# Row maxima of causal attention scores: two full key blocks as one shared score plus the positive part of a difference

## The chip, the cores and the metric

One core of a Trainium2 chip runs the whole program. Its engines are TensorE (PE in the profile, PEld for its weight loads), VectorE (DVE), ScalarE (ACT), GpSimd (POOL) and SyncE (SP, which here issues DMAs). The metric is the device time of one execution in microseconds; the median of three runs is compared.

## The reference

Four layers run on 4096 rows of 128 numbers: a message-passing layer with a recurrent layer behind it, a neighbour average, and a transformer layer with causal attention and a mixture of eight experts. The change is in the attention of the last layer. It has 4 query heads and 2 key heads of width 32, and 4096 positions:

```python
q = q * cos + _rotate_half(q) * sin
k = k * cos + _rotate_half(k) * sin
k = jnp.repeat(k, NREP, axis=1)
scores = jnp.einsum('bhtd,bhsd->bhts', q, k) / jnp.sqrt(jnp.float32(HD))
scores = jnp.where(causal[None, None], scores, jnp.float32(-1e+30))
att = jax.nn.softmax(scores, axis=-1)
```

The softmax needs, for each query and head, the largest score over all keys up to the query.

## The kernel before, in words

The program is a row of phases, each closed before the next begins. Three of them matter here.

`split_heads` (L808) projects the rows to queries and keys, turns them by the position tables, and leaves each head in 16-bit pieces: `T.qs[h]` holds query rows as high, low and high part (96 rows), `T.ks[h]` the key rows as high, high and low part, so that one matmul over 96 rows gives a score of nearly 32-bit accuracy. It runs over 8 groups `g` of 512 positions. For each group PE projects, DVE multiplies by the cosine and sine tables (`turn(g)`, L941 to L949), POOL adds the two products (L988, L990), ACT rounds to 16 bits (L1011, L1013), and DVE subtracts to get the low parts (`lows(g - 1)`, L954 to L962, one group behind). The pieces are put in their rows by DMAs: SP loads the two tables of a group (L861, L862) and issues eight placements of query high parts (L869), ACT those of the key high parts and query low parts (L1016, L1002), POOL those of the key low parts (L983). SP's program is a fixed sequence: the tables of group `g + 2`, which wait for `turn` of group `g`, then the eight placements of group `g`, and so on.

`make_masks` (L1643) follows, with a few instructions.

`row_maxima` (L1025) finds the maxima. Queries go in 32 tiles of 128 (four tiles `k` to each group `g`), and for each tile and each head `h` the keys from the start to the tile's own group go in chunks `c` of two blocks of 512 keys. One (group, tile, head, chunk) is a unit; there are 320, in a fixed order, and each engine's program follows that order. In a unit PE writes one score block of 128 x 512 for each key block (L1066), and for the block of the tile's own group it adds the mask by a further matmul (L1069). DVE then reduces the unit's 512 or 1024 columns to one maximum (L1081). Three PSUM buffers `sc` of two blocks each go round: PE may begin unit `u` when unit `u - 3` is reduced. After the last chunk of the last head of a tile, DVE makes the tile's negated maxima and splits them in two 16-bit halves (L1087, L1092, L1095). Once per group PE transposes these (`flatten`, L1053; that of the previous group comes before tile 1 of a group) and ACT copies the result into two further rows of `T.qs` (L1116). In this phase ACT does nothing else, and POOL works only in its first microseconds (L1106 to L1109).

The last chunk of each unit list is the only one with a mask: in an even group it holds one block (512 columns, two matmuls), in an odd group two blocks (1024 columns, three matmuls). All chunks before it are two full blocks of earlier groups: 1024 columns and two matmuls. There are none of these in groups 0 and 1, one per tile and head in groups 2 and 3, two in groups 4 and 5 and three in groups 6 and 7, 192 of the 320 units in all.

`attend` (L1120) comes next and uses the same queries and keys with exponentials.

Of the kernel before, what the change touches and what calls it, by code (L numbers as in the profile page):

```python
# [807 lines left out]
def split_heads(nc, T):  # L808
# [6 lines left out]
    with Phase(nc, "heads") as ph:  # L815
# [12 lines left out]
        k, ks = ([ph.sb(f"{n}{i}", [P, G]) for i in range(2)] for n in ("k", "ks"))  # L828
# [23 lines left out]
        def _(sp):  # L852
# [52 lines left out]
        def _(dve):  # L905
# [27 lines left out]
            def turn(g):  # L933
                b = g % 2
                dve.wait_ge(tables[b], 32 * (g // 2 + 1))
                dve.wait_ge(q_projected, g + 1)
                if g >= 2:
                    dve.wait_ge(q_low_ready, g - 1)
                    dve.wait_ge(q_high_ready, g - 1)
                    dve.wait_ge(q_ready, g - 1)  # L940
                nc.vector.tensor_tensor(q[b][:, :], q_plain[b][:, :], cos[b][:, :], ALU.mult)  # L941
                nc.vector.tensor_tensor(qs[b][:, :], q_turned[b][:, :], sin[b][:, :], ALU.mult).then_inc(q_turned_by, 1)
                dve.wait_ge(k_projected, g + 1)
                if g >= 2:
                    dve.wait_ge(k_low_ready, g - 1)
                    dve.wait_ge(k_high_ready, g - 1)
                    dve.wait_ge(k_ready, g - 1)
                nc.vector.tensor_tensor(k[b][:, :], k_plain[:, :], cos[b][:, :], ALU.mult)
                nc.vector.tensor_tensor(ks[b][:, :], k_turned[:, :], sin[b][:, :], ALU.mult).then_inc(k_turned_by, 1)  # L949

            def lows(g):
# [10 lines left out]
                nc.vector.tensor_tensor(k_low[b][:, :], k[b][:, :], k_high[b][:, :], ALU.subtract).then_inc(k_low_ready, 1)  # L962
# [8 lines left out]
        def _(pool):  # L971
# [13 lines left out]
            for g in range(NG):  # L985
# [4 lines left out]
                nc.gpsimd.tensor_tensor(k[b][:, :], k[b][:, :], ks[b][:, :], ALU.add).then_inc(k_ready, 1)  # L990
# [5 lines left out]
        def _(act):  # L996
# [7 lines left out]
            for g in range(NG):  # L1004
# [8 lines left out]
                nc.scalar.copy(k_high[b][:, :], k[b][:, :]).then_inc(k_high_ready, 1)  # L1013
# [8 lines left out]
MAX_UNIT = 2.0 ** 15  # L1022


def row_maxima(nc, T):  # L1025
# [3 lines left out]
    with Phase(nc, "maxima") as ph:  # L1029
        sc = [ph.ps(f"sc{i}", [P, 2, G]) for i in range(3)]  # L1030
        flat = ph.ps("flat", [2, NHEAD, G], F16)
        part = ph.sb("part", [P, 2, NHEAD, NG // 2])
# [6 lines left out]
        units = [(g, k, h, c) for g in range(NG) for k in range(TPG) for h in range(NHEAD) for c in range(g // 2 + 1)]  # L1039
        tiles_done = [sum(NHEAD * (g // 2 + 1) * TPG for g in range(t // TPG)) + NHEAD * (t // TPG // 2 + 1) * (t % TPG + 1)  # L1040
# [3 lines left out]
        def _(pe):  # L1044
# [12 lines left out]
            for u, (g, k, h, c) in enumerate(units):  # L1057
# [4 lines left out]
                t = g * TPG + k  # L1062
                for j in range(min(2, g + 1 - 2 * c)):
# [48 lines left out]
        def _(act):  # L1112
            for g in range(NG):
# [3 lines left out]
                last.then_inc(placed, 1)  # L1117

# [554 lines left out]
def program(nc, D, out):  # L1673
    T = Tensors()
    Phase.used.clear()
    with ExitStack() as ctx:
# [41 lines left out]
        with ExitStack() as third:  # L1718
            def sb3(name, shape, dt=F32):
                return third.enter_context(nc.sbuf_tensor(name, shape, dt))  # L1720
# [7 lines left out]
            T.ks = [sb3(f"ks{h}", [P, N], F16) for h in range(NKV)]  # L1728
            T.score_unit = sb3("score_unit", [P, 1])
# [76 lines left out]
```

## Time and profile before

| | us |
|---|---|
| median of 3 runs | 7872.52 |
| lowest and highest run | 7867.58, 7874.14 |
| the profiled execution, its own time | 7870.33 |
| span of that execution in the profile | 7868.3 |
| VectorE busy in it | 5390.5 |
| TensorE busy | 4613.6 |
| ScalarE busy | 2829.4 |

Times in the profile count from the start of the span. The recurrent layer takes most of the span; `split_heads` begins at 6312, `row_maxima` runs from 6393 to 6752 and `attend` follows it. Busy time is the union of an engine's instructions. An instruction's duration is longer than the distance to the next one where two of them overlap, so both are read below: a group's mean gives the duration, a timeline the distance.

### The profile page before, as it was taken

To read this page: it belongs to the slowest core of one execution; us is meant where nothing else is said; L and a number is where in the kernel's file an instruction comes from. 1 tells how busy PE (TensorE), PEld (TensorE's weight loads), DVE (VectorE), ACT (ScalarE), POOL (GpSimd) and SP (SyncE) were. 2 spreads that over 40 slices of the span, in tenths; PEclk is the share of its full clock that TensorE was granted. 3 is DMA by queue.
4 is the path that set the end of the run, shared out by engine and by line. 5 is a ranking of instruction groups with operands and counts; after the bars stand their busy time and mean duration, and the time that the engine had idled before them with its cause. 6 is when DMAs were issued, how large, how long until landed. Compare 5 with 4: busy or idle time off the path is not lost. (4 is left out here: it accounts for less than half of the span.)

```text
span 7868.3 us, 179097 instructions
## 1 busy us (share of the span) xinstructions
PE 4613.6 (59%) x57632; PEld 3119.7 (40%) x57632; DVE 5390.5 (69%) x30690; ACT 2829.4 (36%) x14714; POOL 217.7 (3%) x504
## 2 busy tenths in 40 slices
PE   4555555555555555555555555555446868788799
PEld 3444444444444444444444444444333421344344
DVE  7666666666666666666666666666646679788544
ACT  3333333333333333333333333333320010488333
POOL 0000000000000000000000000000000020000011
PEclk6555555555555555555555555555558975799799
DMA  1000000000000000000000000000004610000000
GB/s 44 14 12 14 14 12 14 14 13 14 14 14 12 14 14 13 14 14 12 14 14 12 14 14 12 14 14 12 2 2 144 200 48 0 2 1 1 24 4 5
DMA packets 93261, 164.29 MB, mean 21 GB/s; under 512 B 8711, under 2 KB 23087, under 8 KB 92337
## 3 DMA queue, kind: packets, MB, share of 16 engines
q1 hardware_dynamic: 89009, 150.47, 6.1%
q8 instruction: 442, 7.24, 0.4%
q14 instruction: 482, 3.95, 0.2%
q10 hardware_dynamic: 2816, 2.10, 0.1%
q0 software_dynamic: 512, 0.53, 0.0%
HBM read 146.25 MB, written 2.10 MB: 19 GB/s over the span
## 5 line engine op out<-in xcount | busy, mean ns | idle before, releaser
L431 PE MATMUL lstm_gates<-lstm_h_parts,lstm_wrec 128*128 128x1 f16 x36864 | 2074.0, 170 | 2822.8 <-DVE lstm_h_parts L576 2814.6
L431 PEld LDWEIGHTS lstm_gates<-lstm_h_parts,lstm_wrec 128*128 128x128 f16 x36864 | 1615.6, 107 | 3425.4 <-DVE lstm_h_parts L576 3414.3
L487 ACT ACTIVATE lstm_tanhs<-lstm_gates 128x3 f32<-128x3 f32 x4096 | 707.5, 173 | 2726.2 <-PE lstm_gates L431 2726.0
L431 PE MATMUL lstm_gate_o<-lstm_h_parts,lstm_wrec 128*128 128x1 f16 x12288 | 1440.7, 165 | 0.0
L576 DVE SCALAR_TENSOR_TENSOR lstm_h_parts<-lstm_tanh_o,lstm_c_pair 128x1 f16<-128x1 f32 x4096 | 645.5, 158 | 912.8 <-ACT lstm_c_pair L493 912.8
L571 DVE SCALAR_TENSOR_TENSOR lstm_terms<-lstm_tanhs 128x2 f32<-128x2 f32 x4096 | 655.1, 160 | 765.9 <-ACT lstm_tanhs L487 546.1
L595 DVE RECIPROCAL lstm_rec<-lstm_dist 128x52 f32<-128x52 f32 (+1 forms) x2560 | 1171.6, 462 | 4.2 <-issue 4.2
L493 ACT ACTIVATE lstm_c_pair<-lstm_c_pair 128x1 f32<-128x1 f32 x4096 | 639.0, 156 | 951.4 <-DVE lstm_terms L571 951.4
L431 PEld LDWEIGHTS lstm_gate_o<-lstm_h_parts,lstm_wrec 128*128 128x128 f16 x12288 | 961.2, 104 | 0.0
L454 PE MATMUL lstm_acc<-msg,lstm_wt 128*128 128x128 f32 x2048 | 780.9, 488 | 38.2 <-DVE lstm_wt L603 38.2
L582 DVE TENSOR_TENSOR lstm_h_parts<-hid_t,lstm_h_parts 128x1 f16<-128x1 f32 x4096 | 667.5, 163 | 179.9 <-DVE hid_t L578 13.1
L490 ACT ACTIVATE lstm_tanh_o<-lstm_gate_o 128x1 f32<-128x1 f32 x4096 | 679.9, 166 | 0.0
L585 DVE TENSOR_SCALAR lstm_tanhs<-lstm_c_pair 128x1 f32<-128x1 f32 x4096 | 622.1, 152 | 7.4 <-issue 7.4
L578 DVE SCALAR_TENSOR_TENSOR hid_t<-lstm_tanh_o,lstm_c_pair 128x1 f32<-128x1 f32 x4096 | 608.3, 149 | 0.0
L571 DVE DVE_READ_ACCUMULATOR lstm_terms<-lstm_tanhs 128x1 f32 x4096 | 580.1, 142 | 0.0
L454 PEld LDWEIGHTS lstm_acc<-msg,lstm_wt 128*128 128x128 f32 x2048 | 512.2, 312 | 41.0 <-DVE lstm_wt L603 21.4
L1081 DVE TENSOR_REDUCE maxima_part<-maxima_sc 128x1 f32<-128x1024 f32 (+1 forms) x320 | 331.2, 1109 | 6.5 <-PE maxima_sc L1069 6.1
L1303 DVE TENSOR_TENSOR attend_low<-xn_t,attend_high 128x1024 f16<-128x1024 f32 (+1 forms) x288 | 324.2, 1162 | 6.3 <-ACT attend_high L1259 1.4
L1254 ACT ACTIVATE xn_t<-attend_sc 128x1024 f32<-128x1024 f32 (+1 forms) x288 | 281.3, 983 | 117.9 <-PE attend_sc L1184 71.1
L1066 PE MATMUL maxima_sc<-ks,qs 96*128 96x512 f16 x576 | 263.7, 565 | 68.8 <-DVE maxima_part L1081 38.8
L603 DVE SCALAR_TENSOR_TENSOR lstm_wt<-lstm_dist,lstm_sens 128x128 f32<-128x128 f32 x1024 | 294.9, 291 | 4.6 <-issue 4.6
L1486 PE MATMUL experts_up<-experts_f,experts_w 128*128 128x512 f16 (+1 forms) x1152 | 280.3, 389 | 23.2 <-DVE experts_hidden L1606 22.6
(260 smaller groups left out, 4626.0 us busy)
## 6 DMA issues: line engine op xcount, KB each, us to landing
lstm_ring<-in_adj SPq DMA_DIRECT2D x256, 256.0 KB, 2.7
gnn_ring<-in_adj SPq DMA_DIRECT2D x64, 1024.0 KB, 5.2
w<-in_w SPq DMA_DIRECT2D x2, 1364.0 KB, 9.5
heads_cos<-in_cos SPq DMA_DIRECT2D x8, 256.0 KB, 3.1
heads_sin<-in_sin SPq DMA_DIRECT2D x8, 256.0 KB, 3.5
qs<-heads_q_high SPq DMA_DIRECT2D x64, 32.0 KB, 2.3
out<-x SPq DMA_DIRECT2D x8, 256.0 KB, 2.3
ks<-heads_k_high ACTq DMA_DIRECT2D x16, 64.0 KB, 2.6
```

The costliest lines, as they stand in the source:

```text
L431: return nc.tensor.matmul(o, wrec[:, w, g, :], h_parts[:, (n - 1) % NH, k:k + 1], start=False, stop=True, skip_group_check=True)
L454: nc.tensor.matmul(acc[t % 2][:, :], wt[:, q % 2, r, :], T.msg[:, (q % QPT) * QUAD + r, :], start=first, stop=True, skip_group_check=True) ...
L487: nc.scalar.activation(tanhs[:, 0:3], gates[t % 2][:, i, :], ACT.Tanh, scale=unscale).then_inc(tanhs_ready, 1)
L490: nc.scalar.activation(tanh_o[:, :], gate_o[t % 2][:, i:i + 1], ACT.Tanh, scale=unscale).then_inc(tanh_o_ready, 1)
L493: nc.scalar.activation(tanh_c, c_twice, ACT.Tanh, scale=0.5).then_inc(tanh_c_ready, 1)
L571: nc.vector.scalar_tensor_tensor(out=terms[:, :], in0=tanhs[:, 0:2], scalar=1.0, in1=tanhs[:, 2:4], op0=ALU.add, op1=ALU.mult, accum_out=c ...
L576: nc.vector.scalar_tensor_tensor(out=h_parts[:, n % NH, 0:1], in0=tanh_o[:, :], scalar=1.0, in1=tanh_c, op0=ALU.add, op1=ALU.mult).then_in ...
L578: nc.vector.scalar_tensor_tensor(out=T.hid_t[:, n:n + 1], in0=tanh_o[:, :], scalar=1.0, in1=tanh_c, op0=ALU.add, op1=ALU.mult).then_inc(fu ...
L582: nc.vector.tensor_tensor(h_parts[:, n % NH, 1:2], T.hid_t[:, n:n + 1], h_parts[:, n % NH, 0:1], ALU.subtract).then_inc(low_ready, 1)
L585: nc.vector.tensor_scalar(tanhs[:, 3:4], c_twice, 0.5, None, ALU.mult).then_inc(c_kept, 1)
L595: nc.vector.reciprocal(rec[:, q % 2, c], dist[:, q % 3, c]).then_inc(rec_ready, 1)
L1081: nc.vector.reduce_max(part[:, k % 2, h, c:c + 1], sc[u % 3][:, 0:w, :].rearrange("p a s -> p (a s)"), AX.X).then_inc(reduced, 1)
```

## The change

Of two full key blocks `a` and `b` the larger of two scores is written as `sb + max(0, q(ka - kb))`. `split_heads` makes the key differences `d = ka - kb` of the block pairs (0,1), (2,3) and (4,5), splits them in a 16-bit high and low part and places them in a new tensor `T.kd`, laid out as `T.ks`. To have the key of the group before at hand, the key buffer goes from 2 to 3. In `row_maxima` PE scores, in the 192 full units, the difference block and the block `b`; ACT takes the positive part of the first into one of three new buffers `more`; DVE adds the second to it and takes the maximum in one instruction. The masked units stay as they were. ACT's copies of the flattened maxima are put between its new instructions.

In `split_heads`:

```diff
+            def place_difference(p):
+                c = slice(p * G, (p + 1) * G)
+                sp.wait_ge(d_low_ready, p + 1)
+                for h in range(NKV):
+                    sp.dma_start(T.kd[h][0:2 * HD, c], d_high[2 * h * HD:2 * (h + 1) * HD, :]).then_inc(d_placed, 16)
+                    sp.dma_start(T.kd[h][rows(2), c], d_low[rows(2 * h), :]).then_inc(d_placed, 16)
             for g in range(NG):
                 if g + 2 < NG:
                     load_tables(g + 2)
                 place(g)
+                if g % 2 == 0 and 1 <= g // 2 <= NPAIR:
+                    place_difference(g // 2 - 1)
+            sp.wait_ge(d_placed, 16 * 2 * NKV * NPAIR)
...
-                nc.vector.tensor_tensor(k[b][:, :], k_plain[:, :], cos[b][:, :], ALU.mult)
+                nc.vector.tensor_tensor(k[g % 3][:, :], k_plain[:, :], cos[b][:, :], ALU.mult)
...
+                p = g // 2
+                if b and p < NPAIR:
+                    if p >= 1:
+                        dve.wait_ge(d_placed, 16 * 2 * NKV * p)
+                    nc.vector.tensor_tensor(d[:, :], k[(g - 1) % 3][:, :], k[g % 3][:, :], ALU.subtract).then_inc(d_ready, 1)
+                    dve.wait_ge(d_ready, p + 1)
+                    nc.vector.tensor_copy(d_high[:, :], d[:, :]).then_inc(d_high_ready, 1)
+                    dve.wait_ge(d_high_ready, p + 1)
+                    nc.vector.tensor_tensor(d_low[:, :], d[:, :], d_high[:, :], ALU.subtract).then_inc(d_low_ready, 1)
```

In `row_maxima` (`NPAIR` is 3, `LOWEST` is -3e38):

```diff
+        doubled = [2 * c + 1 < g for g, k, h, c in units]
...
+                if doubled[u]:
+                    nc.tensor.matmul(sc[u % 3][:, 0, :], T.qs[h][0:K, t * P:(t + 1) * P], T.kd[h // 2][0:K, c * G:(c + 1) * G],
+                                     start=True, stop=True)
+                    nc.tensor.matmul(sc[u % 3][:, 1, :], T.qs[h][0:K, t * P:(t + 1) * P],
+                                     T.ks[h // 2][0:K, (2 * c + 1) * G:(2 * c + 2) * G],
+                                     start=True, stop=True).then_inc(scored, 1)
+                    continue
...
-                nc.vector.reduce_max(part[:, k % 2, h, c:c + 1], sc[u % 3][:, 0:w, :].rearrange("p a s -> p (a s)"),
-                                     AX.X).then_inc(reduced, 1)
+                if doubled[u]:
+                    dve.wait_ge(more_ready, sum(doubled[:u + 1]))
+                    m = more[(sum(doubled[:u + 1]) - 1) % 3][:, :]
+                    nc.vector.tensor_tensor_reduce(out=m, in0=m, in1=sc[u % 3][:, 1, :], scale=1.0, scalar=LOWEST, op0=ALU.add, op1=ALU.max,
+                                                   accum_out=part[:, k % 2, h, c:c + 1]).then_inc(reduced, 1)
+                else:
+                    nc.vector.reduce_max(part[:, k % 2, h, c:c + 1], sc[u % 3][:, 0:w, :].rearrange("p a s -> p (a s)"),
+                                         AX.X).then_inc(reduced, 1)
...
+            pairs = [u for u in range(len(units)) if doubled[u]]
+            place(0)
+            for n, u in enumerate(pairs):
+                g, k, h, c = units[u]
+                if (k, h, c) == (2, 0, 0):
+                    place(g - 1)
+                act.wait_ge(scored, u + 1)
+                if n >= 3:
+                    act.wait_ge(reduced, pairs[n - 3] + 1)
+                nc.scalar.activation(more[n % 3][:, :], sc[u % 3][:, 0, :], ACT.Relu).then_inc(more_ready, 1)
+            place(NG - 1)
```

`place(g)` is ACT's old loop body: the wait for `flatten(g)` and four copies.

## Rows read from the trace of the kernel before

**Rows 1.** The page: busy time of each engine, its share of the span, instructions.
```profile
PE 4613.6 (59%) x57632; PEld 3119.7 (40%) x57632; DVE 5390.5 (69%) x30690; ACT 2829.4 (36%) x14714; POOL 217.7 (3%) x504
```
**Rows 2.** Stretches of row_maxima, groups 1, 2, 3, 6, 7: length, busy PE, PEld, DVE, ACT, POOL (instructions), clock, DMA.
```profile
6411.20:6431.60 20.40, 14.70 (x64) 4.50 (x62) 20.00 (x28) 2.00 (x4) 0.00 (x0) 0.92 0.00 1
6431.60:6461.60 30.00, 23.99 (x82) 5.94 (x81) 29.52 (x43) 2.00 (x4) 0.00 (x0) 0.77 0.00 0
6461.60:6500.70 39.10, 31.97 (x97) 7.93 (x95) 38.51 (x47) 2.00 (x4) 0.00 (x0) 0.70 0.00 1
...
6605.60:6672.00 66.40, 59.56 (x144) 11.23 (x145) 65.99 (x77) 2.00 (x4) 0.00 (x0) 0.55 0.00 0
6672.00:6747.70 75.70, 66.33 (x157) 13.77 (x155) 74.84 (x79) 2.00 (x4) 0.00 (x0) 0.55 0.00 0
```
**Rows 3.** Who waited for whom, 6410 to 6748: us in total, times, longest.
```profile
ACT qs L1116 <- PE maxima_flat L1053: 302.5, 7, 66.9
PEld maxima_sc L1066 <- DVE maxima_part L1081: 242.3, 287, 1.8
...
DVE maxima_part L1081 <- PE maxima_sc L1066: 0.4, 1, 0.4
```
**Rows 4.** DVE's timeline in row_maxima: start, us, line, shapes, count (merged).
```profile
6398.92 2.48 DVE L1081 TENSOR_REDUCE maxima_part<-maxima_sc 128x1 f32<-128x512 f32 x4
...
6411.16 3.49 DVE L1081 TENSOR_REDUCE maxima_part<-maxima_sc 128x1 f32<-128x1024 f32 x3
```
**Rows 5.** Groups by line and shape, 6300 to 7400: count, busy us, mean ns, idle before.
```profile
L1081 DVE TENSOR_REDUCE maxima_part<-maxima_sc 128x1 f32<-128x1024 f32 x256 | 295.2, 1216 | 0.4 <-PE maxima_sc L1066 0.4
...
L1254 ACT ACTIVATE xn_t<-attend_sc 128x512 f32<-128x512 f32 x32 | 19.1, 598 | 7.4 <-PE attend_sc L1188 7.4
...
L1301 DVE CAST attend_high<-xn_t 128x512 f16<-128x512 f32 x16 | 6.7, 422 | 0.0
...
L941 DVE TENSOR_TENSOR heads_q<-heads_q_plain,heads_cos 128x512 f32<-128x512 f32 x8 | 5.5, 688 | 8.7 <-DMA heads_sin<-in_sin 4.4 <-PE heads_q_turned L892 4.4
...
L962 DVE TENSOR_TENSOR heads_k_low<-heads_k,heads_k_high 128x512 f16<-128x512 f32 x8 | 5.4, 679 | 0.0
```
**Rows 6.** A timeline in the recurrent layer: an instruction with an accumulator, and the next engine.
```profile
3000.40 0.16 DVE L571 SCALAR_TENSOR_TENSOR lstm_terms<-lstm_tanhs 128x2 f32<-128x2 f32 x1
3000.48 0.14 DVE L571 DVE_READ_ACCUMULATOR lstm_terms<-lstm_tanhs 128x1 f32 x1
3000.66 0.16 ACT L493 ACTIVATE lstm_c_pair<-lstm_c_pair 128x1 f32<-128x1 f32 x1 [0.23 <-DVE lstm_terms L571]
```
**Rows 7.** Timeline of group 0, DVE behind PE (0.50 clock), and one unit of group 1.
```profile
6394.74 0.69 DVE L1081 TENSOR_REDUCE maxima_part<-maxima_sc 128x1 f32<-128x512 f32 x1 [0.16 <-PE maxima_sc L1069]
...
6395.60 0.69 DVE L1081 TENSOR_REDUCE maxima_part<-maxima_sc 128x1 f32<-128x512 f32 x1 [0.16 <-PE maxima_sc L1069]
...
6412.44 0.60 PE L1066 MATMUL maxima_sc<-ks,qs 96*128 96x512 f16 x2 [0.73 <-DVE maxima_part L1081]
```
**Rows 8.** Timelines around the flattening, groups 1 and 7: PE, ACT, DVE.
```profile
6413.20 1.05 PE L1053 MATMUL maxima_flat<-ident,maxima_halves 128*2 128x128 f16 x16
...
6414.29 2.00 ACT L1116 COPY qs<-maxima_flat 2x512 f16<-2x512 f16 x4 [38.29 <-PE maxima_flat L1053]
...
6690.96 0.17 DVE L1095 SCALAR_TENSOR_TENSOR maxima_halves<-maxima_neg,maxima_halves 128x4 f16<-128x4 f32 x1
6691.51 2.36 DVE L1081 TENSOR_REDUCE maxima_part<-maxima_sc 128x1 f32<-128x1024 f32 x2 [0.38 <-PE maxima_sc L1066]
...
6747.80 1.87 PE L1053 MATMUL maxima_flat<-ident,maxima_halves 128*2 128x128 f16 x16 [2.54 <-DVE maxima_halves L1095]
```
**Rows 9.** split_heads: SP's only wait for another engine, SP's last issues, DVE's first wait for tables, the next phase.
```profile
SPq L860 <- DVE heads_ks L949: 19.4, 1, 19.4
...
6368.64 15.40 SPq L869 DMA_DIRECT2D qs<-heads_q_high  x24
...
6359.25 0.69 DVE L941 TENSOR_TENSOR heads_q<-heads_q_plain,heads_cos 128x512 f32<-128x512 f32 x1 [2.23 <-DMA heads_sin<-in_sin]
...
6386.04 0.11 DVE L1652 MEMSET ident<- 128x64 uint32 x1 [8.08 <-PEq L62]
```

More of the change, by code:

```diff
@@ L827, in split_heads @@
         q, qs = ([ph.sb(f"{n}{i}", [P, G]) for i in range(2)] for n in ("q", "qs"))
-        k, ks = ([ph.sb(f"{n}{i}", [P, G]) for i in range(2)] for n in ("k", "ks"))
+        k, ks = ([ph.sb(f"{n}{i}", [P, G]) for i in range(m)] for n, m in (("k", 3), ("ks", 2)))
+        d = ph.sb("d", [P, G])
+        d_high, d_low = ph.sb("d_high", [P, G], F16), ph.sb("d_low", [P, G], F16)
+        d_ready, d_high_ready, d_low_ready, d_placed = (ph.sem(n) for n in ("d_ready", "d_high_ready", "d_low_ready", "d_placed"))
         q_high, q_low = ([ph.sb(f"{n}{i}", [P, G], F16) for i in range(2)] for n in ("q_high", "q_low"))
@@ L944, in turn @@
                 if g >= 2:
-                    dve.wait_ge(k_low_ready, g - 1)
-                    dve.wait_ge(k_high_ready, g - 1)
                     dve.wait_ge(k_ready, g - 1)
-                nc.vector.tensor_tensor(k[b][:, :], k_plain[:, :], cos[b][:, :], ALU.mult)
+                if g >= 3:
+                    dve.wait_ge(k_low_ready, g - 2)
+                    dve.wait_ge(k_high_ready, g - 2)
+                    dve.wait_ge(d_ready, min((g - 1) // 2, NPAIR))
+                nc.vector.tensor_tensor(k[g % 3][:, :], k_plain[:, :], cos[b][:, :], ALU.mult)
                 nc.vector.tensor_tensor(ks[b][:, :], k_turned[:, :], sin[b][:, :], ALU.mult).then_inc(k_turned_by, 1)
@@ L961, in lows @@
                 dve.wait_ge(k_high_ready, g + 1)
-                nc.vector.tensor_tensor(k_low[b][:, :], k[b][:, :], k_high[b][:, :], ALU.subtract).then_inc(k_low_ready, 1)
+                nc.vector.tensor_tensor(k_low[b][:, :], k[g % 3][:, :], k_high[b][:, :], ALU.subtract).then_inc(k_low_ready, 1)
+                p = g // 2
[7 more added lines that the diff above has]
+                    nc.vector.tensor_tensor(d_low[:, :], d[:, :], d_high[:, :], ALU.subtract).then_inc(d_low_ready, 1)
             for g in range(NG):
@@ L989, in _ @@
                 pool.wait_ge(k_turned_by, g + 1)
-                nc.gpsimd.tensor_tensor(k[b][:, :], k[b][:, :], ks[b][:, :], ALU.add).then_inc(k_ready, 1)
+                nc.gpsimd.tensor_tensor(k[g % 3][:, :], k[g % 3][:, :], ks[b][:, :], ALU.add).then_inc(k_ready, 1)
                 if g >= 1:
@@ L1012, in _ @@
                 act.wait_ge(k_ready, g + 1)
-                nc.scalar.copy(k_high[b][:, :], k[b][:, :]).then_inc(k_high_ready, 1)
+                nc.scalar.copy(k_high[b][:, :], k[g % 3][:, :]).then_inc(k_high_ready, 1)
                 act.wait_ge(k_high_ready, g + 1)
@@ L1022 @@
 MAX_UNIT = 2.0 ** 15
+NPAIR = (NG - 1) // 2
+LOWEST = -3e38
 def row_maxima(nc, T):
@@ L1031, in row_maxima @@
         flat = ph.ps("flat", [2, NHEAD, G], F16)
+        more = [ph.sb(f"more{i}", [P, G]) for i in range(3)]
+        more_ready = ph.sem("more_ready")
         part = ph.sb("part", [P, 2, NHEAD, NG // 2])
@@ L1112, in _, with place @@
         def _(act):
-            for g in range(NG):
+            def place(g):
                 act.wait_ge(flat_ready, g + 1)
@@ L1728, in program @@
             T.ks = [sb3(f"ks{h}", [P, N], F16) for h in range(NKV)]
+            T.kd = [sb3(f"kd{h}", [P, NPAIR * G], F16) for h in range(NKV)]
             T.score_unit = sb3("score_unit", [P, 1])
```

## The prediction

> **What bounds the kernel now.** Over the whole span VectorE is busiest at 69% [rows 1], but that is an average over phases with different limits, and the change touches two of them. So I read the stretches of `row_maxima`, group by group. DVE is busy for 98 to 99% of each (74.84 of 75.70 us in group 7) while ACT has four copies, 2.00 us [rows 2]. The waits say the same from the other side: between 6410 and 6748 PE's weight loads waited 242.3 us for reductions, DVE's reductions 0.4 us for PE's scores, and ACT sat idle for 302.5 us [rows 3]. VectorE sets the pace here and ScalarE is free.
>
> The second thing to see is the distance between reductions, not their duration. Three of 1024 columns end 3.49 us after the first began and one lasts 1.216 us [rows 4, 5], so the distance is (3.49 - 1.22) / 2 = **1.135 us**. Four of 512 columns take 2.48 us at 0.69 each [rows 4, 7]: distance (2.48 - 0.69) / 3 = **0.60 us**. This rebuilds group 7: per tile and head four units of 1024 columns, 16 times, 16 x 4 x 1.135 = 72.6 us, and four tile ends of about 0.6 us give 75.0 of the measured 75.7.
>
> The third is TensorE's clock: mean 0.92 in group 1, 0.77, 0.70, and 0.55 in groups 6 and 7 [rows 2], that is, first nearly always at 2.4 GHz, then mostly at 1.2. At the lower level a unit of two matmuls costs PE 0.855 us: the two reductions of group 0 that wait for PE start 6395.60 - 6394.74 = 0.86 apart, 0.43 per matmul. At the upper level two matmuls are over in 0.60 us [rows 7].
>
> In `split_heads` SP is the limit from 6335 on: its queue waited once for another engine, and its last 24 placements run to 6384 without a gap; the next phase starts at 6386, when they have landed [rows 9].
>
> **The change part by part.** *DVE in the 192 full units.* Out goes a reduction of 1024 columns at 1.135 us. In comes one instruction over 512 columns with one operand from PSUM and one from SBUF, and a maximum to hand out. No such instruction is in the trace. Nearest for its body is the product of a PSUM and an SBUF tile of that size, 0.688 us long [rows 5], which is the duration of a 512-column reduction, so I give it that one's distance, 0.60. For the maximum handed out, the nearest row is the recurrent layer's accumulator read: a second DVE instruction, begun 0.08 us after the first, 0.14 long [rows 6]. I take 0.08, the distance; the bounds are nothing (the value leaves with the body) and 0.23 (body and read both run to their ends before the next: 0.69 + 0.14 = 0.83). So 0.68 us, and 192 x (1.135 - 0.68) = **-87.4 us**, with ends -102.7 and -58.6.
>
> *ACT.* The positive part of 512 PSUM columns is priced by the exponential of that size and output type, 0.598 us [rows 5]. Bounds: 0.48 (distance of its small copies, (2.00 - 0.57) / 3 [rows 8]) and 0.62 or so. It lies under DVE's 0.68, beside it. It is no bound of its own, but DVE now waits for ACT, and ACT for PE.
>
> *The ring of three buffers.* What is late next is that chain. PE's two matmuls 0.60, ACT 0.60, DVE until its maximum is out 0.60 + 0.14 = 0.74, and three handovers of 0.04 (the read ends at 3000.62, ACT starts at 3000.66 [rows 6]) make 2.06 us, in which three units pass. Three full units at DVE's pace are 2.04, two and one masked unit of 512 columns 1.96, two and one of 1024 columns 2.50. So per tile and head the ring adds about 0.05 us in group 2, 0.1 in groups 4 and 6, 0.03 in 7 and nothing in 3 and 5: 16 x 0.28 = **+5 us**. Before, the ring was slack.
>
> *Flattening and copies.* PE's 16 transposes (1.05 us at the upper level, 1.87 at the lower) already let DVE wait 0.38 us in group 7 [rows 8]; with the ring tight I expect about 1 us each in groups 2 to 7, 0.6 more than now: **+4 us**. ACT's four copies (2.00 us) now stand between its positive parts. They begin when the last full unit of a tile is through; DVE then still has that unit (0.68), the masked one (0.60 or 1.135) and the tile's end (0.6) before it: 1.9 to 2.4 us against 2.0 for copies and 0.6 for the next positive part. 0.2 to 0.7 is uncovered, six times: **+3 us**.
>
> *The clock.* The number of matmuls is unchanged. If PE stood at the lower level throughout, groups 2 to 7 (4, 5, 6, 7, 8 and 9 matmuls per tile and head) would cost it 16 x 39 x 0.427 = 266.5 us, against 213.8 us for DVE's new units (16 times 1.28, 1.815, 1.96, 2.495, 2.64 and 3.175). So where the clock is low, PE becomes the bound: 53 us if always. Group 1, where PE does three matmuls in each 1.135 us, ran at 0.92, group 7 with nine in 4.54 us at 0.55 [rows 2]. After the change group 7 has nine in 3.2 us, nearer to group 1's work than to its own of now, so I take group 1's 0.92, which is 16% of the time at the lower level: 0.16 x 53 = **+8 us**.
>
> *`split_heads`.* SP gets 12 more placements behind the query ones. Its last 24 took 15.40 us, 0.64 each [rows 9], nothing hides them, since SP's queue is the phase's limit: **+7.7 us**, with ends of 0 (if a queue pays for the transfers, not for their number) and 15 (if the tables queued behind them come late for DVE and it costs as much again). SP's new wait for the low part finds it made; what is queued behind it, the tables of the next group but two, has waited for DVE in any case. DVE gets 3 x (0.68 + 0.42 + 0.68) = 5.3 us of differences [rows 5]; they hide behind SP, for DVE waits 4.4 us for tables in all [rows 5], 2.23 of it in group 4 [rows 9]. Without that cover they would cost up to 5 us. The third key buffer removes no wait that shows.
>
> *Sum.* -87.4 + 5 + 4 + 3 + 8 + 7.7 = -59.7 us. From the profiled execution's own 7870.3 that is 7810.6. The median of the runs lies 2.2 us above that execution, so 7812.8: **7813 us**. The unknown read cost alone moves it from about 7800 (the ring then takes back part of the gain) to 7842.
>
> **The rivals.** *The clock stays down.* PE still pauses between units, waiting for a buffer, and a clock that stays at 1.2 GHz makes PE the bound: 266.5 us and six flattenings of 1.87, 278 us for groups 2 to 7, which now last 6747.7 - 6431.6 = 316.1 us [rows 2]. That is -38, with +7.7 -30: **7842 us**, and up to 15 more with imperfect overlap. For it: groups 6 and 7 stand at 0.55 with PE busy for 88 to 90% of the time [rows 2]. Against it: a bound PE would pause no more, and group 1 has 0.92. The Trainium skill's page "TensorE: Matmul & The Clock Gate", section "A second HAM failure mode: psum-queue depth-cycling", says that short idles between matmul groups that go round PSUM buffers let the clock fall and rise again; groups 2 and 3 with 0.77 and 0.70 agree with that. Chance 0.17.
>
> *The new instruction goes through its columns at half the rate* (slower). Two sources, an addition and a running maximum might take two cycles a column. Then its body has the distance of 1024 columns, 1.135, and the read's 0.08 on top: 192 x 0.08 = +15, and with the placements' 7.7 +23: **7895 us**. The change turns to a loss from a distance of about 1.135 - 7.7 / 192 = 1.095 us. Against it: the two-source product and the one-source reduction of 512 columns take the same 0.68 to 0.69 us [rows 5, 7]; for it: neither of those does both. Chance 0.09. The Trainium skill's "Vector Engine (DVE) Microarchitecture Reference", section "Points that are easy to get wrong", halves the rate of a form with two 32-bit sources in SBUF; here one is in PSUM, so by its letter the rule does not bite, and no row here shows the case.
>
> **How the numbers follow.** The forecast, with its bounds, has 0.74. A measurement of this kernel can tell about 0.2%, 16 us, from no change, so faster means under 7857. That holds for the forecast (0.73; 0.01 within) and most of the clock's case (0.14; 0.03 within); of the half rate 0.08 is slower and 0.01 within. Faster 0.87, same 0.05, slower 0.08. The range goes from 7785 (read for nothing, clock at the upper level, the small terms gone: -102.7 + 10 + 7.7 = -85) to 7853, which takes in most of the clock's case and leaves out the half rate.
>
> **What would show it.** Right: `split_heads` ends about 8 us later; groups 2 to 7 last some 248 us in place of 316; the new DVE instruction stands 0.68 to 0.72 us apart; clock of 0.9 there; DVE's idle time is put down to ACT. Wrong: distances over 0.85 us, or a clock near 0.55 with DVE waiting for PE behind ACT, or ACT's positive part at over 0.7 us, which would make the ring, not DVE, the bound.

## The result and the profile after

| | before | after |
|---|---|---|
| median of six runs each, us | 7870.85 | 7798.76 |
| lowest and highest run | 7865.7, 7874.14 | 7796.64, 7806.16 |
| span of the profiled execution | 7868.3 | 7794.7 |

The ratio is 0.991, with a 95% interval from 0.9898 to 0.9923. The forecast was 7813 us, with a range from 7785 to 7853: right in sign and range, and 14 us too cautious.

The first question is where the 73.6 us of span went. I take the limits from VectorE's timeline: `split_heads` from its first reduction (6314.91 before, 6312.10 after) to the first instruction of `make_masks`, and `row_maxima` from its first reduction to its last 16-bit half. `split_heads` went from 71.1 to 78.6 us (+7.5), `row_maxima` from 353.7 to 276.8 (-76.9), and all the rest of the program together by -4.2; over the profiles of the runs below that rest varies by 9 us (7438 to 7447, the run with sixteen extra instructions left out), so 4.2 says nothing. Inside `row_maxima`, from one group's last half to the next's:

| group | 2 | 3 | 4 | 5 | 6 | 7 | sum |
|---|---|---|---|---|---|---|---|
| before, us | 30.3 | 38.6 | 48.5 | 56.8 | 66.3 | 75.3 | 316.0 |
| after, us | 27.2 | 30.6 | 37.8 | 40.9 | 46.7 | 55.5 | 238.7 |

On the page, over the whole span, little seems to happen (to be read against [rows 1]): VectorE lost 88 us, ScalarE gained 113.

```profile
PE 4526.7 (58%) x57609; PEld 3112.5 (40%) x57632; DVE 5302.8 (68%) x30891; ACT 2942.5 (38%) x14906; POOL 217.1 (3%) x504
```

The stretches of groups 1, 2, 3, 6 and 7 answer to [rows 2], columns as there. Two things are to be seen: the clock (third from the right), which was 0.55 in groups 6 and 7 and is now 1.00 and 0.94, and DVE's busy time, which is no longer 98% everywhere. In group 2 it is 22.23 of 27.20, in group 6 42.33 of 46.80, while in group 3 it is still 30.15 of 30.60.

```profile
6416.20:6436.80 20.60, 14.42 (x66) 4.43 (x65) 20.14 (x28) 2.60 (x5) 0.00 (x0) 1.00 0.00 1
6436.80:6464.00 27.20, 22.99 (x81) 6.50 (x81) 22.23 (x61) 11.46 (x20) 0.00 (x0) 0.81 0.00 0
6464.00:6494.60 30.60, 22.85 (x94) 6.05 (x95) 30.15 (x61) 12.16 (x21) 0.00 (x0) 1.00 0.00 1
...
6573.20:6620.00 46.80, 38.83 (x142) 8.30 (x144) 42.33 (x126) 30.10 (x52) 0.00 (x0) 1.00 0.00 1
6620.00:6675.50 55.50, 41.05 (x152) 11.05 (x154) 51.13 (x124) 29.05 (x51) 0.00 (x0) 0.94 0.00 1
```

The waits between 6410 and 6690 answer to [rows 3]. PE's weight loads still wait for VectorE, but there is a new line: VectorE itself now waits for ScalarE, 53 times and 16.8 us in all.

```profile
PEld maxima_sc L1093 <- DVE maxima_part L1120: 64.0, 118, 2.0
...
DVE maxima_more L1120 <- ACT maxima_more L1171: 16.8, 53, 1.3
```

The groups by line and shape answer to [rows 5]: 192 of the 256 reductions of 1024 columns are gone, and in their place stand VectorE's new instruction (a custom operation in the profile), its accumulator read, and ScalarE's positive part at 597 ns (the exponential that served for its price took 598).

```profile
L1120 DVE CUSTOM_DVE_ANT_0 maxima_more<-maxima_more,maxima_sc 128x512 f32<-128x512 f32 x192 | 125.3, 683 | 17.3 <-ACT maxima_more L1171 16.8 <-PE maxima_sc L1095 0.4
L1171 ACT ACTIVATE maxima_more<-maxima_sc 128x512 f32<-128x512 f32 x192 | 112.8, 597 | 126.6 <-PE maxima_sc L1095 124.9 <-DVE maxima_part L1120 0.8
...
L1123 DVE TENSOR_REDUCE maxima_part<-maxima_sc 128x1 f32<-128x1024 f32 x64 | 77.0, 1219 | 0.3 <-PE maxima_sc L1105 0.3
...
L1120 DVE DVE_READ_ACCUMULATOR2_ANT maxima_part<- 128x1 f32 x192 | 15.8, 82 | 0.0
```

The distance, the number on which the prediction hung, is in VectorE's timeline of group 7 (start, duration). The three custom instructions of one tile and head start at 6661.19, 6661.81 and 6662.42: **0.61 us apart**, 0.605 over longer runs. The read begins at the same time as the next body and lies wholly beside it. This answers to [rows 4], where the distance was 1.135, and to [rows 6].

```profile
6661.19 0.69 DVE L1120 CUSTOM_DVE_ANT_0 maxima_more<-maxima_more,maxima_sc 128x512 f32<-128x512 f32 x1
6661.81 0.08 DVE L1120 DVE_READ_ACCUMULATOR2_ANT maxima_part<- 128x1 f32 x1
6661.81 0.68 DVE L1120 CUSTOM_DVE_ANT_0 maxima_more<-maxima_more,maxima_sc 128x512 f32<-128x512 f32 x1
...
6662.42 0.68 DVE L1120 CUSTOM_DVE_ANT_0 maxima_more<-maxima_more,maxima_sc 128x512 f32<-128x512 f32 x1
```

In `split_heads` the answer to [rows 9] is SP's timeline: the last four difference placements (0.64 to 0.66 from start to start) stand ahead of the last eight query placements, which end at 6388.69, and the next phase starts 2.0 us later, as before.

```profile
6381.02 0.61 SPq L878 DMA_DIRECT2D kd<-heads_d_high  x1
6381.68 0.61 SPq L879 DMA_DIRECT2D kd<-heads_d_low  x1
6382.32 0.61 SPq L878 DMA_DIRECT2D kd<-heads_d_high  x1
6382.97 0.59 SPq L879 DMA_DIRECT2D kd<-heads_d_low  x1
6383.61 5.08 SPq L872 DMA_DIRECT2D qs<-heads_q_high  x8
...
6390.70 0.11 DVE L1707 MEMSET ident<- 128x64 uint32 x1 [9.83 <-PEq L62]
```

Last, the new wait, in one turn of group 6 with the clock at its upper level (all engines, in order of time). A turn is the time from a head's first full unit to the next head's. VectorE starts the first full unit of a head at 6590.65; its maximum is out when the read ends, at 6591.35. That frees the buffer of the masked unit, and PE starts it at 6591.40. VectorE starts the second full unit at 6591.27, and its read ends at 6591.95. That frees the buffer of the next head's first full unit, and PE starts it at 6592.01: its weight load (PEld) had been waiting for VectorE. Its two matmuls are over at 6592.62. ScalarE starts at 6592.65 and needs 0.60 for the first of its three; VectorE starts the next head's first full unit at 6593.39.

```profile
6590.65 0.69 DVE L1120 CUSTOM_DVE_ANT_0 maxima_more<-maxima_more,maxima_sc 128x512 f32<-128x512 f32 x1 [0.23 <-ACT maxima_more L1171]
...
6591.27 0.68 DVE L1120 CUSTOM_DVE_ANT_0 maxima_more<-maxima_more,maxima_sc 128x512 f32<-128x512 f32 x1
...
6591.40 0.39 PE L1102 MATMUL maxima_sc<-ks,qs 96*128 96x512 f16 x1 [0.32 <-DVE maxima_part L1120]
...
6591.63 0.38 PE L1105 MATMUL maxima_sc<-future_keys,ident 128*128 128x512 bf16 x1
6591.87 0.08 DVE L1120 DVE_READ_ACCUMULATOR2_ANT maxima_part<- 128x1 f32 x1
...
6592.01 0.10 PEld L1093 LDWEIGHTS maxima_sc<-kd,qs 96*128 96x128 f16 x1 [0.49 <-DVE maxima_part L1120]
6592.01 0.39 PE L1093 MATMUL maxima_sc<-kd,qs 96*128 96x512 f16 x1
...
6592.24 0.38 PE L1095 MATMUL maxima_sc<-ks,qs 96*128 96x512 f16 x1
...
6592.65 1.81 ACT L1171 ACTIVATE maxima_more<-maxima_sc 128x512 f32<-128x512 f32 x3 [0.93 <-PE maxima_sc L1095]
...
6593.39 0.69 DVE L1120 CUSTOM_DVE_ANT_0 maxima_more<-maxima_more,maxima_sc 128x512 f32<-128x512 f32 x1 [0.23 <-ACT maxima_more L1171]
```

So a turn takes 6593.39 - 6590.65 = **2.74 us**: 0.62 to VectorE's second full unit, 0.68 until that one's maximum is out, 0.06 to PE, 0.61 for two matmuls, 0.03, 0.60 ScalarE, 0.14 to VectorE. VectorE's own work in it is 3 x 0.605 + 0.60 = 2.415. In group 4, where a head has one full unit fewer, the buffer is that of the first full unit, the 0.62 falls away, and the turn is 2.14 us against 1.81 of own work. My first theory for the experiments was that the waits which VectorE now has come from this chain (with the copies and the flattening as small extras), and the 7.5 us in `split_heads` from SP's issue time; the rivals were a chain that doesn't matter beside the clock, and transfers or VectorE's differences as the cause in `split_heads`.

### The profile page after: what moved, and what is told of

Same layout as the page of the kernel before. It is cut to its first block and busy times, and to the rows that moved or that the text cites. A ratio compares the mean times of both kernels' runs of the same rounds, so it can differ in the third digit from the quotient of the medians.

```text
span 7794.7 us, 179835 instructions
## 1 busy us (share of the span) xinstructions
PE 4526.7 (58%) x57609; PEld 3112.5 (40%) x57632; DVE 5302.8 (68%) x30891; ACT 2942.5 (38%) x14906; POOL 217.1 (3%) x504
## 5 line engine op out<-in xcount | busy, mean ns | idle before, releaser
L1309 ACT ACTIVATE xn_t<-attend_sc 128x1024 f32<-128x1024 f32 (+1 forms) x288 | 281.2, 983 | 119.1 <-PE attend_sc L1239 72.8
L1661 DVE SCALAR_TENSOR_TENSOR experts_hidden<-experts_up,experts_unscale,experts_silu 128x512 f32<-128x512 f32 (+1 forms) x192 | 143.7, 750 | 191.2 <-ACT experts_silu L1602 190.5
L502 ACT ACTIVATE lstm_dist<-lstm_ring,tiny 128x256 f32<-128x256 f32 x512 | 256.1, 503 | 7.3 <-DVE lstm_scale L555 6.5
```

## The experiments

Single profiled runs of one and the same `row_maxima` give groups 2 to 7 as 238.7, 239.9 and 236.6 us (the changed kernel twice, and the run with POOL's placements below), so differences of up to 3.3 us in that sum decide nothing; the distances in a timeline do.

**`split_heads` alone.** The differences are made and placed, the whole of `row_maxima` is that of before, and nothing reads `T.kd`. The core of it:

```diff
-                if doubled[u]:
-                    dve.wait_ge(more_ready, sum(doubled[:u + 1]))
...
+                nc.vector.reduce_max(part[:, k % 2, h, c:c + 1], sc[u % 3][:, 0:w, :].rearrange("p a s -> p (a s)"),
+                                     AX.X).then_inc(reduced, 1)
```

> The key differences are made and placed, but the maxima are found as before, so nobody reads them. Theory (SP's queue is the limit of split_heads and 12 further placements at 0.62 to 0.64 us each lie on its end): make_masks begins 7.6 us later after split_heads began than in the kernel before (before: 51 us from SP's third table load at 6334.98 to 6386.04), and row_maxima lasts what it lasted before (353.7 us from the first reduction to the last halves). Rival (the placements lie beside the others and the 7.6 us of the changed kernel come from the new waits of DVE and of row_maxima's start): under 3 us.

Measured: 7880.2 us beside 7867.8 for the kernel before on the same chip. `split_heads` took 78.3 us (+7.2), groups 2 to 7 317.5 us against 316.0. The cost of the new placements is there without any of the new work in `row_maxima`, and the gain is all in the other half of the change. The other 5 of the 12.4 us lie in phases that have not changed and within their spread. `split_heads` has a spread of its own: in the seven profiles with the new placements on SP it takes 77.9 to 81.2 us.

**One wait instead of two.** In a full unit VectorE waits for ScalarE only, which itself has waited for PE.

```diff
-                dve.wait_ge(scored, u + 1)
+                if not doubled[u]:
+                    dve.wait_ge(scored, u + 1)
```

> DVE's new instruction waits for ScalarE's positive part alone, not for the scores as well (ScalarE itself waits for both scores). Rival theory (the 0.14 to 0.17 us between ScalarE's end and DVE's start, against 0.04 in the recurrent layer, is the price of the second wait): the handover falls to about 0.05 and groups 2 to 7, 238.7 us in the changed kernel, fall by about 4 to 235. Theory (the handover is no matter of the second wait): handover 0.14 to 0.17, groups 2 to 7 within 1.5 us of 238.7.

Measured: 7804.0 us; groups 2 to 7 235.8 us, 0.8 below the lowest of the three sums named above. The time decides nothing here, but the timeline of group 6 does (ScalarE's first of three ends 0.60 after its start, at 6594.52):

```profile
6591.92 0.69 DVE L1121 CUSTOM_DVE_ANT_0 maxima_more<-maxima_more,maxima_sc 128x512 f32<-128x512 f32 x1 [0.53 <-ACT maxima_more L1172]
...
6593.92 1.81 ACT L1172 ACTIVATE maxima_more<-maxima_sc 128x512 f32<-128x512 f32 x3 [1.17 <-PE maxima_sc L1095]
...
6594.55 0.69 DVE L1121 CUSTOM_DVE_ANT_0 maxima_more<-maxima_more,maxima_sc 128x512 f32<-128x512 f32 x1
```

The handover from ScalarE to VectorE fell from 0.14 to 0.03 us, and the turn from 2.74 to 2.63. The turn shortens by just what the handover lost, which it can only do if that chain sets it. The theory that the second wait doesn't matter is refuted.

**ScalarE waits for its own block.** PE reports the difference block by itself, so ScalarE starts one matmul earlier.

```diff
                     nc.tensor.matmul(sc[u % 3][:, 0, :], T.qs[h][0:K, t * P:(t + 1) * P], T.kd[h // 2][0:K, c * G:(c + 1) * G],
-                                     start=True, stop=True)
+                                     start=True, stop=True).then_inc(diffed, 1)
...
-                act.wait_ge(scored, u + 1)
+                act.wait_ge(diffed, n + 1)
```

> ScalarE waits for the difference score alone, so that PE's second matmul leaves the chain. Theory (of the 25 us by which groups 2 to 7 exceed DVE's own work of 213.8, some 17 are the chain PE, ScalarE, DVE through three score buffers): the chain is 0.22 us shorter at the upper clock, the period of a tile and head in group 6 falls from 2.74 to about 2.52, groups 2 to 7 last about 228 us. Rival (PE's clock or the flattening and copies hold DVE up, not the chain): 237 to 239 us.

Measured: 7787.6 us beside 7867.8; groups 2 to 7 230.7 us, 6 to 9 less than the three runs of the unchanged code, more than their spread. The turn in group 6 is 6610.08 - 6607.55 = 2.53 us, 0.21 shorter, and in the turn shown above a unit's second matmul ends 0.22 behind its first (6592.62 and 6592.40), which is what left the chain:

```profile
6607.55 0.69 DVE L1120 CUSTOM_DVE_ANT_0 maxima_more<-maxima_more,maxima_sc 128x512 f32<-128x512 f32 x1
...
6610.08 0.69 DVE L1120 CUSTOM_DVE_ANT_0 maxima_more<-maxima_more,maxima_sc 128x512 f32<-128x512 f32 x1
```

**PE starts on ScalarE's release as well.** The difference block of a buffer is free once ScalarE has read it; PE may refill that half before VectorE is done with the other.

```diff
-                if u >= 3:
+                early = doubled[u] and u >= 3 and doubled[u - 3]
+                if early:
+                    pe.wait_ge(more_ready, sum(doubled[:u - 2]))
+                elif u >= 3:
                     pe.wait_ge(reduced, u - 2)
...
+                    if early:
+                        pe.wait_ge(reduced, u - 2)
```

> As the run before it, and PE writes a difference score as soon as ScalarE has read the one three units back, without waiting for DVE's reduction of that unit, where both are full units. Theory (chain through the score buffers): groups 4 and 6 lose most of what is left, groups 2 to 7 last about 224 us. Rival (clock, flattening, copies): no better than the kernel as changed, 237 to 239 us.

Measured, with the edit before it included: 7787.5 us, groups 2 to 7 230.4 us. The 224 us expected did not come: there is no gain over the run before. One part of the reason stands in the timeline of group 6, where full units follow each other at 0.85 us while the granted clock is 0.50:

```profile
6598.10 0.69 DVE L1125 CUSTOM_DVE_ANT_0 maxima_more<-maxima_more,maxima_sc 128x512 f32<-128x512 f32 x1 [0.41 <-ACT maxima_more L1176]
...
6598.95 0.69 DVE L1125 CUSTOM_DVE_ANT_0 maxima_more<-maxima_more,maxima_sc 128x512 f32<-128x512 f32 x1 [0.16 <-ACT maxima_more L1176]
...
6599.80 0.69 DVE L1125 CUSTOM_DVE_ANT_0 maxima_more<-maxima_more,maxima_sc 128x512 f32<-128x512 f32 x1 [0.16 <-ACT maxima_more L1176]
```

0.85 us for two matmuls is PE at 1.2 GHz ([rows 7] have 0.86): in such stretches no chain matters, since PE itself is the bound. The releaser named is ScalarE, because it comes last, but PE was late. In this run the clock stood at 0.81 to 0.90 in groups 2, 4, 6 and 7. Why it was lower here than in other runs isn't settled.

The other part is that the edit had less to take than expected. Where the clock stood at 1.00 it did what the theory says: in group 4 the turn fell from 1.92 us with ScalarE's own block to 1.82, VectorE's own work being 1.81 (the first full units of two heads, one behind the other):

```profile
6496.30 0.68 DVE L1125 CUSTOM_DVE_ANT_0 maxima_more<-maxima_more,maxima_sc 128x512 f32<-128x512 f32 x1
...
6498.11 0.68 DVE L1125 CUSTOM_DVE_ANT_0 maxima_more<-maxima_more,maxima_sc 128x512 f32<-128x512 f32 x1
```

In group 6 it fell from 2.53 to 2.43 or 2.52, and in group 7 it stayed at 3.06, since the chain there runs by way of a masked unit, for which PE still waits for VectorE. Twelve turns in group 4 and four in group 6 at 0.10 each make an estimated 1.6 us, too little to be seen in the sum beside slow turns.

**Copies spread out.** The four copies of a flattening go one by one between the positive parts of tile 2, the changed kernel otherwise.

```diff
-                if (k, h, c) == (2, 0, 0):
-                    place(g - 1)
+                if k == 2 and c == 0:
+                    place_head(g - 1, h)
```

> ScalarE's four copies of the flattened maxima are done one before each head's first positive part in the third tile of a group, not all four before the first. Theory (four copies in a row make DVE wait 0.8 us in groups 2, 4 and 6 and up to 0.3 in group 7): groups 2 to 7 fall by 2 to 3 us from 238.7. Rival (ScalarE has no room for any copy, and the wait only moves from one place to four): within 1 us of 238.7.

Measured: 7796.3 us beside 7873.7; groups 2 to 7 233.2 us, 3.5 to 6.8 less than the three runs of the unchanged code. In the changed kernel VectorE lost 0.86 us behind the copies in groups 2, 4 and 6 and 0.33 in group 7. Now ScalarE's timeline shows each copy where it was idle before, and these losses are 0.07. That makes 2.6 us, as expected; the rest of the fall from 238.7 is not shown to be the copies' (the mean clock was 0.98 here and 0.95 there).

```profile
6592.27 1.81 ACT L1176 ACTIVATE maxima_more<-maxima_sc 128x512 f32<-128x512 f32 x3 [0.93 <-PE maxima_sc L1095]
6594.10 0.57 ACT L1159 COPY qs<-maxima_flat 2x512 f16<-2x512 f16 x1
6595.01 1.81 ACT L1176 ACTIVATE maxima_more<-maxima_sc 128x512 f32<-128x512 f32 x3 [0.34 <-PE maxima_sc L1095]
```

**POOL places the differences.** The twelve placements move from SP's program to POOL's, behind its low key parts.

```diff
-                    sp.dma_start(T.kd[h][0:2 * HD, c], d_high[2 * h * HD:2 * (h + 1) * HD, :]).then_inc(d_placed, 16)
-                    sp.dma_start(T.kd[h][rows(2), c], d_low[rows(2 * h), :]).then_inc(d_placed, 16)
+                    pool.dma_start(T.kd[h][0:2 * HD, c], d_high[2 * h * HD:2 * (h + 1) * HD, :]).then_inc(d_placed, 16)
+                    pool.dma_start(T.kd[h][rows(2), c], d_low[rows(2 * h), :]).then_inc(d_placed, 16)
```

> The 12 placements of key differences are issued by POOL behind its key placements, not by SP. Theory (SP's queue is the limit, POOL's has room): make_masks begins 7 to 8 us earlier than in the kernel as changed, as early as before the change within 1 us; row_maxima is as in the changed kernel, 277 us. Rival (POOL's additions of queries come late behind its wait for the difference, and DVE, PE and ScalarE with them): split_heads gains under 3 us or loses.

Measured: 7792.6 us; `split_heads` 74.4 us, 4.2 less than in the changed kernel but 3.2 more than before, where "within 1 us" was expected. SP's last issue ends at 6384.44, 70.1 us after the phase's first reduction (69.1 before, 76.6 in the changed kernel), so SP's time is back. But the next phase starts 4.2 us after that and not 2.0. The timeline of all engines shows who came late instead:

```profile
6376.71 0.50 POOL L1005 DMA_DIRECT2D kd<-heads_d_low  x1
...
6377.23 1.27 POOL L1010 TENSOR_TENSOR heads_q<-heads_q,heads_qs 128x512 f32<-128x512 f32 x1
...
6378.61 0.62 ACT L1035 CAST heads_q_high<-heads_q 128x512 f16<-128x512 f32 x1 [5.94 <-POOL heads_q L1010]
...
6381.60 5.12 ACTq L1026 DMA_DIRECT2D qs<-heads_q_low  x8
...
6388.66 0.11 DVE L1707 MEMSET ident<- 128x64 uint32 x1 [6.25 <-PEq L62]
```

POOL's additions of the last group stand behind its four placements, ScalarE's rounding behind those additions, and ScalarE's last eight placements behind that: they end at 6386.72, and 1.94 us later the next phase starts. The bound had moved from SP's queue to ScalarE's. Neither forecast held: the gain lies between the theory's 7 to 8 us and the rival's 3, and the late additions are the rival's.

**All of these together** (ScalarE's own block, PE's early start, copies spread out, POOL's placements); the diff is that of the four.

> ScalarE waits for its own block alone, PE writes difference scores early, the copies are spread and POOL issues the placements. Theory: the gains add up: split_heads 7.6 us shorter, groups 2 to 7 at about 222 us, in all 7775 to 7780 us. Rival (each only moves the wait to the next thing): over 7788 us.

Measured: 7777.2 us beside 7873.7, as the theory said; groups 2 to 7 222.2 us. `split_heads` took 74.4 us, 4.2 less than in the changed kernel in place of 7.6, as with POOL's placements alone. What PE's early start adds to the 222.2 no run without it shows. VectorE's own work there is 213.8: per tile and head 1.205, 1.74, 1.81, 2.345, 2.415 and 2.95 us at the paces 0.605, 0.60 and 1.135, 16 times, and 24 tile ends of 0.6. VectorE's wait for ScalarE has gone from 16.8 to 0.6 us:

```profile
DVE maxima_more L1125 <- PE maxima_sc L1100: 1.0, 3, 0.4
DVE maxima_more L1125 <- ACT maxima_more L1181: 0.6, 4, 0.2
```

**The disputed price by itself.** Behind the end of `row_maxima`, in the version with all edits and the later placements of the next run, VectorE gets four more instructions each of four forms: a sum, a sum with its maximum handed out, and both again with `more[1]` in place of the PSUM tile. The first two:

```diff
+            for e in range(4):
+                nc.vector.tensor_tensor(extra[e][:, :], more[0][:, :], sc[2][:, 1, :], ALU.add).then_inc(priced, 1)
+            dve.wait_ge(priced, 4)
+            for e in range(4):
+                nc.vector.tensor_tensor_reduce(out=extra[e][:, :], in0=more[0][:, :], in1=sc[2][:, 1, :], scale=1.0,
+                                               scalar=LOWEST, op0=ALU.add, op1=ALU.max, accum_out=most[:, e:e + 1]).then_inc(priced, 1)
```

> Sixteen extra DVE instructions of 512 columns stand at the end of the maxima, four of each form, and only the distance between their starts is read. First theory (the accumulator read costs no distance, the body keeps the pace of 0.60): the sum of an SBUF and a PSUM tile without a maximum stands 0.60 us apart, and the same with the maximum handed out 0.60 to 0.61. Second theory (the read does cost its 0.08, and the body by itself is faster): without the maximum 0.52 to 0.53 apart, with it 0.60 to 0.61. For both sources in SBUF, the rule of half rate would give 1.1 us apart with a maximum, full rate 0.60. The time as a whole should stand 9 to 12 us above the run beside it.

Measured, in VectorE's timeline: the plain sums take 2.47 for four, so (2.47 - 0.69) / 3 = 0.59 us apart; with the maximum handed out the starts run from 6658.73 to 6660.56 in three steps, 0.61 apart; with both sources in SBUF from 6661.29 to 6663.13, 0.61, and the plain sum of these 0.60 ((2.50 - 0.69) / 3).

```profile
6656.22 2.47 DVE L1150 TENSOR_TENSOR maxima_extra<-maxima_more,maxima_sc 128x512 f32<-128x512 f32 x4
6658.73 0.69 DVE L1153 CUSTOM_DVE_ANT_0 maxima_extra<-maxima_more,maxima_sc 128x512 f32<-128x512 f32 x1
...
6660.56 0.68 DVE L1153 CUSTOM_DVE_ANT_0 maxima_extra<-maxima_more,maxima_sc 128x512 f32<-128x512 f32 x1
...
6661.29 0.69 DVE L1157 CUSTOM_DVE_ANT_0 maxima_extra<-maxima_more 128x512 f32<-128x512 f32 x1
...
6663.13 0.68 DVE L1157 CUSTOM_DVE_ANT_0 maxima_extra<-maxima_more 128x512 f32<-128x512 f32 x1
```

So the body has the distance of the plain sum, and handing out the maximum adds 0.01 to 0.02 us to it, not 0.08. The time as a whole, 7782.3 us, stands 5.7 above the median of the next run, the same kernel without these sixteen, where 9 to 12 were expected; in the timeline they take 10.1 us.

**Placements behind the additions.** In the version with all edits, POOL's placements of a pair come behind its additions of the next group, where it waits 1.45 us for the low key part anyway.

```diff
                 nc.gpsimd.tensor_tensor(k[g % 3][:, :], k[g % 3][:, :], ks[b][:, :], ALU.add).then_inc(k_ready, 1)
+                if g % 2 and g >= 3:
+                    place_difference((g - 3) // 2)
                 if g >= 1:
                     place_low(g - 1)
-                if g % 2 == 0 and 1 <= g // 2 <= NPAIR:
-                    place_difference(g // 2 - 1)
```

> The version with all edits, but POOL's placements of the differences come behind its additions of the next group, where POOL waits 1.45 us for the low keys anyway. First theory (in the run with POOL's placements the last ScalarE placements came 1.5 us late, since POOL's additions stood behind its placements): the query and key phase takes 71 to 73 us, as before the change, the maxima 259 to 261, the time is 7774 to 7777, ratio 0.988 to before. Rival (the rest of the 3 us is the shared transfer queues, however the placements are ordered): the phase stays at 74 to 75, the time at 7777.

Measured: **7776.6 us**, four runs from 7775.0 to 7779.7; ratio to the kernel before 0.9885, 95% interval 0.9869 to 0.9901. `split_heads` took 72.8 us, 1.7 more than before the change, with all the new transfers in it, and 71.7 in the run above, which has the same placements; that speaks against shared transfer queues as its limit. `row_maxima` took 261.4 us. ScalarE's last eight placements start 65.8 us after the phase's first reduction in place of 67.3 (62.3 before the change) and still end behind SP's last.

**The changed kernel again**, beside it on the same chip.

> The changed kernel as it is, run beside the version with all edits and the kernel before on the same chip: 7796 to 7806 us, ratio 0.990 to 0.992. All theories expect the same; it gives the difference to the version with all edits, 20 us or so, its interval.

Measured: 7798.4 us, five runs from 7797.3 to 7802.2; ratio to before 0.9913, interval 0.9899 to 0.9927. The version with all edits is 21.8 us faster, and no run of the one reaches a run of the other: it beats both kernels. Against the single run of the version with POOL's earlier placements (7777.2) its time can't be told apart; only the phase can: 74.4 us in both profiles with the earlier placements, 72.8 and 71.7 in those with the later ones.

## Why the prediction was right, and by how much it was off

**VectorE bounds, and its distance counts: right.** Taking the full units from 1.135 us to a shorter distance is what made the gain; `split_heads` alone has none of it. The total is 14 us off, as much as the price of the new instruction is by itself; that the 4.5 us by which the waits came out larger and the 4.2 us of unchanged phases cancel is luck.

**The price of the new instruction: the step that was off.** The prediction took "0.08, the distance" for the maximum handed out, from the recurrent layer's read [rows 6], with "nothing" as one bound. The bound came out: 0.605 us with the maximum handed out, for a body taken at 0.60. But [rows 6] don't show the price of a read. The 0.08 there is the distance from a body of two columns to its read, and small instructions stand as far apart in that layer with no read between them:

```profile
3000.85 0.16 DVE L576 SCALAR_TENSOR_TENSOR lstm_h_parts<-lstm_tanh_o,lstm_c_pair 128x1 f16<-128x1 f32 x1 [0.22 <-ACT lstm_c_pair L493]
3000.92 0.15 DVE L578 SCALAR_TENSOR_TENSOR hid_t<-lstm_tanh_o,lstm_c_pair 128x1 f32<-128x1 f32 x1
```

What an instruction behind a read pays for it can't be seen there, since VectorE waits for ScalarE until 3000.85. After the change it can: with 512 columns in each body the read starts together with the next body and runs beside it. The term is 192 x (1.135 - 0.605) = -101.8 us in place of -87.4. For that bound the prediction had about 7800 us, and 7798.8 came.

**The waits in `row_maxima`: right in kind, too small.** Groups 2 to 7 shrank by 77.3 us, so 101.8 - 77.3 = 24.5 us came back, where ring, flattening, copies and clock were to bring 5 + 4 + 3 + 8 = 20. I summed over VectorE's timeline by how much each distance exceeds its pace: 17.6 us ahead of and between full units (ring and clock, 13 predicted), 2.4 after the flattening (4), 2.7 after the copies (3); 1.8 of the 24.5 I could not place.

The ring's chain was sized nearly right, at 2.06 us. Measured from the start of a full unit to that of the third behind it, it is 0.70 for VectorE with its read, 0.05, 0.61 for two matmuls, 0.03, 0.60 for ScalarE and 0.14, together 2.13; only the last handover, to the instruction with two awaited semaphores, is far from the 0.04 assumed. What failed is what the chain was held against. At 0.68 a unit, two full units and a masked one of 512 columns take VectorE 1.96; at the measured 0.605 they take 1.81. So 0.32 us is lost per turn in groups 4 and 6, not 0.1. And in group 7 the chain was started from a full unit, where it starts from the masked one: PE may refill that buffer only when its reduction of 1.22 us is over, and 0.32 us is lost in two turns of three, where 0.03 was expected.

Most of the 17.6 us is the ring. Inside the tiles of the changed kernel, group 6 has twelve turns of 2.74 us, group 4 ten of 2.14, group 7 six of 3.27 and group 2 three of 1.52; the same numbers recur in the other runs of this `row_maxima`, and each fell by 0.11 with one wait and by 0.21 or 0.22 with ScalarE's own block. Over VectorE's own work (2.415, 1.81, 2.95 and 1.205) that is an estimated 11.7 us if the slower turns of these places hold as much, in place of 5. The other 6 are left for the clock (8 predicted) and for the starts of tiles. Two turns of group 4 stand at a granted clock of 0.50 and take 2.56 us, PE's six matmuls at 0.43: there it was the clock.

**The clock: right in its level.** Weighted by their lengths, groups 2 to 7 had a mean of 0.95 (0.92 predicted), from the windows of the profile, 0.81 in group 2 to 1.00 in groups 3, 5 and 6. The rival of a clock that stays down would have shown 0.55 and PE as the bound. The Trainium skill's "TensorE: Matmul & The Clock Gate", section "A second HAM failure mode: psum-queue depth-cycling", expects the clock to swing where matmul groups go round PSUM buffers with short idles. The trace agrees: the clock swings (0.81 in group 2 next to 1.00 in group 3, and 0.85 us between units in the run with PE's early start), but it is at the lower level for little of the time. What sets one group apart from the other no run here shows. What the clock cost in all, 8 us in the prediction, no run measures by itself.

**The rival of half rate: wrong.** It needed 1.135 us, and the distance is 0.605. The Trainium skill's "Vector Engine (DVE) Microarchitecture Reference", section "Points that are easy to get wrong", halves the rate of one form with two sources in SBUF that aren't bf16. No run here shows that form; the one measured here, another one, ran at 0.61 us per 512 columns with both sources in SBUF too.

**`split_heads`: right.** +7.7 predicted, +7.5 measured, +7.2 with that half alone; with the spread of 77.9 to 81.2 us, against one profile before, that the numbers meet to 0.2 is luck, but SP's issues show the mechanism. That VectorE's differences are hidden was right as well: once the placements left SP's queue, most of the loss was gone, with the differences still being made.

**The sum.** -59.7 predicted. With -101.8, +24.5 and +7.5 it is -69.8, and -4.2 come from the rest of the program, which the change doesn't touch and which varies by 9 us between the profiles. That is -74.0, beside the 73.6 of span.

## What to carry to other kernels

A distance between two rows is the price of the first of them: what an extra instruction costs is read from the start of the one behind it, and only where nothing else holds that one up. When work is handed from one engine to two in a row, write down the whole turn, buffer by buffer: which unit held the buffer before, when that one lets it go, and what every engine does from there. Then hold it against the pace at the low bound of the new price too, for a faster engine makes the same chain dearer. And a queue that is unloaded shows the next one: after moving transfers, see which engine's last issue the next phase now waits for.

## What the runs showed of the hardware that was not expected

- The sum of two tiles of 512 columns with a running maximum handed out stands 0.61 us apart, the plain sum 0.59 to 0.60, whether one source is in PSUM or both are in SBUF; the profile shows the read as an instruction of its own, 0.08 us long, beside the next body.
- From ScalarE's end to VectorE's start it is 0.14 us when VectorE's instruction waits for two semaphores and 0.03 when it waits for one.
- A DMA placement of this kind takes 0.64 to 0.66 us from start to start on SP's queue and 0.49 to 0.56 on POOL.
- After the change, with PE's weight loads still waiting for VectorE between units, the granted clock of groups 6 and 7 went from 0.55 to 1.00 and 0.94.
